# The Vector engine's order in a Mamba-style layer with a following feed-forward layer: the bias of B and C moved ahead of both weightings of x

## The chip, the cores and the metric

One core of one Trainium2 chip. The time is device time in microseconds (us) of the whole kernel. Engines: PE (TensorE), DVE (VectorE), ACT (ScalarE), POOL (GpSimd), SP (the queue that issues DMAs here).

## What is computed

The input is x of shape (8, 512, 128), fp32. Two residual blocks follow each other:

```
x = x + layernorm(attn(layernorm(x)))
x = x + layernorm(ffn(layernorm(x)))

attn: proj = x @ W_in  ->  z (256), x_raw (512), B (2*64), C (64), dt, lambda, theta
      x_raw = silu(x_raw);  B, C = rms(B)*bias_B, rms(C)*bias_C;  B, C rotated by cumulated angles
      xg = lam*dt * x_raw           (own token)
      xb = (1-lam)*dt*alpha * x_raw of the token before
      chunked state-space sum over 32 heads: scores C.B inside a chunk, a carried state between chunks
      y = rms(y * silu(z));  out = y @ W_out
ffn:  token-shift mixes of x; r = sigmoid(xr@W_r), k = relu(xk@W_k)**2, out = r * (k@W_v)
```

## The kernel before, in words

The eight sequences are cut into chunks of 64 tokens, and two sequences share the 128 partitions, so the work is 32 tiles: tile n is chunk n // 4 of the pair n % 4. A tile depends on tile n-4 through the carried state `st`. The order on each engine is written out by hand: each engine runs its own program, one `step(n, ...)` after the other from n = -2 (PE from -1) to 31, and the engines meet only through semaphores. Steps of different tiles are interleaved: in step n the core of tile n is computed, while tiles n+1 and n+2 are prepared and tile n-1 is finished. The feed-forward block of the chunk two to four back is spread over the steps as well (the functions called `ffn`).

**PE in step n** (lines 1163 to 1182): `project_x(n + 1)` (three matmuls of 512 columns, line 859, into bank 1 `x_ps`; it waits until DVE has made `xg` of tile n from that bank), `turn(n + 1)` (line 923; transposes the rotated B and C, and waits for `mask(n)` of DVE), `project_bc(n + 2)` (three matmuls of 448 columns, line 851, into bank 0 `zbc_ps`: B, C, z), `y_turn(n - 1)` (line 1045; waits for DVE's `y` and, through `o_sb`, for ACT's `late_o` of tile n-2), `mix(n)` (lines 946, 952, 958; needs `x1` and `xg` of tile n), `score(n + 1)` (line 937), `y_out(n - 1)` (line 1054), and a part of the feed-forward block.

**ACT in step n** (lines 700 to 717): `late_o(n - 2)` (lines 686, 688), `x_gate(n + 1)` (line 660: silu of `x_ps` in place, as soon as line 859 is through), `turned(n + 1)`, `copy_in(n + 3)`, a part of the feed-forward block, `late_yt(n - 1)` (line 676), `squares(n + 2)` (lines 649, 651: the sums of squares of B and C; it waits for `bc_ready` of tile n+2, so that ACT and DVE do not read bank 0 at once), `rstd_of`, `z_gate(n + 2)` (line 666), `late_ysq(n - 1)`; then `ffn`, for n % 4 = 1 the four `normed` of line 724.

**POOL in step n**: `lower_part(n + 3)`, a part of the feed-forward block, `early(n + 2)` (lines 450, 453: from the sums of squares to the reciprocal root), `token_factors(n + 2)` (line 461: the factors `wx` of both weightings), `decayed_z(n + 2)` (line 468), `state(n)` (line 476).

**DVE in step n** (lines 1552 to 1571, where the change is): `mask(n)` (line 1378), `gated_y(n - 1)` (line 1397), `state(n - 1)` (line 1386), a part of the feed-forward block, then the first weighting of x of tile n+1 (`x1`, line 1371, which waits for the silu of line 660 and for `wx`), the bias of B and C of tile n+2 (`bc`, line 1354, which waits for line 851), the second weighting of tile n+1 (`xg`, line 1371, the same bank, no further wait), and `rotations(n + 2)` (lines 1359 and 1364). The bias of tile 0 runs before all steps. Between the first steps stand pieces of the preparation: after step 0 `sine_cosine_angles(1)` (lines 1312, 1315, 1316), after step 2 `mixing_weights` (lines 1344 to 1350), and before step 4 a wait for ACT's last sines (line 1589).

Two branches of the program exist; the inputs take `tiles(False)`. After tile 31 the rest of the feed-forward block runs alone (`last_ffn`).

Of the kernel before, what the change touches and what calls it, by code (L numbers as in the profile page):

```python
# [86 lines left out]
def build(nc, x, w_in, a_log, dt_bias, bc_bias, w_out, w_r, w_k, w_v, mu, consts, out, force_general=False):  # L87
    ctx = ExitStack()
    with ctx:  # L89
# [122 lines left out]
        def within(n):  # L212

            return not isinstance(n, int) or 0 <= n < NT
# [15 lines left out]
        def carries(i):  # L230

            return not isinstance(i, int) or i < NT - NQ
# [76 lines left out]
        def lo(u):  # L309
            return UNITS[u][0]  # L310
# [22 lines left out]
        def n_of(u):  # L333
            return hi(u) - lo(u)
# [8 lines left out]
        def column2(i):  # L343

            return i // NQ % 2 * 2 * NQ + i % NQ

        def column3(i):
            return column2(i) + NQ
# [4 lines left out]
        for u2, u3 in ((7, -1), (8, -1), (-1, 5), (-1, 6), (-1, 7), (-1, 8)):  # L353
            first, n = (column2(lo(u2)), n_of(u2)) if u2 >= 0 else (column3(lo(u3)), n_of(u3))
# [845 lines left out]
        def _(dve):  # L1200
# [151 lines left out]
            def biased(n):  # L1352
                dve.wait_ge(S["zbc_ps"], n + 1)
                vec.tensor_tensor(bc[:], zbc_ps[:, 0:G3 * N], bcb_sb[:], ALU.mult).then_inc(S["bc_ready"], 1)  # L1354

            def rotations(n, q):
                dve.wait_ge(S["bc_ready"], n + 1)

                vec.tensor_tensor(rot[:], bc[:].rearrange("p (g a n) -> p g a n", g=G3, a=2).unsqueeze(3)  # L1359
                                  .broadcast_to([128, G3, 2, 2, H]),  # L1360
                                  at(cs_all, n).rearrange("p (a j n) -> p a j n", a=2, j=2).unsqueeze(1)
                                  .broadcast_to([128, G3, 2, 2, H]), ALU.mult).then_inc(S["rotated"], 1)
                dve.wait_ge(S["rotated"], n + 1)
                vec.tensor_tensor(turned_bc[:, q].rearrange("p g (j n) -> p g j n", j=2), rot[:, :, 0], rot[:, :, 1],
                                  ALU.add).then_inc(S["bc_turned"], 1)

            def weighted_x(n, par, a):
                if a == 0:
                    dve.wait_ge(S["x_silu"], n + 1)
                    dve.wait_ge(S["w_ready"], n + 1)  # L1370
                vec.tensor_tensor((x1, xg)[a][:, par].rearrange("p (a e) -> p a e", e=P),  # L1371
                                  x_ps[:].rearrange("p (a e) -> p a e", e=P),
                                  wx[:, par, a].unsqueeze(2).broadcast_to([128, H * R, P]),
                                  ALU.mult).then_inc(S[("x1_ready", "xg_ready")[a]], 1)

            def mask(n):
                dve.wait_ge(S["sg_ps"], n + 1)
                vec.tensor_tensor(sg[:], scores.unsqueeze(1).broadcast_to([128, 2, R, L]),
                                  c_("masks").rearrange("p (a m) -> p a m", a=2).unsqueeze(2)
                                  .broadcast_to([128, 2, R, L]), ALU.mult).then_inc(S["sg_ready"], 1)  # L1380

            def state(i, q):
                dve.wait_ge(S["p_ps"], i + 1)
                dve.wait_ge(S["sg_ps"], i + 2)
                dve.wait_ge(S["st_ready"], i)
                vec.tensor_tensor(sp[:], p_ps, st[:, q], ALU.add).then_inc(S["p_added"], 1)  # L1386

            def gated_y(n, q, par, general):
                dve.wait_ge(S["y_ps"], n + 1)
                dve.wait_ge(S["zec_ready"], n + 1)  # L1390
                if not isinstance(n, int) or n >= 2:
                    dve.wait_ge(S["yt_ps"], n - 1)
                    dve.wait_ge(S["ysq_done"], n - 1)
                if general:
                    vec.tensor_tensor(yk[:], y_ps[par], yk[:], ALU.add).then_inc(G["own"], 1)
                    dve.wait_ge(G["own"], n + 1)
                vec.tensor_tensor(y[:, par], yk[:] if general else y_ps[par], zs[:, q], ALU.mult).then_inc(S["y_ready"], 1)
# [98 lines left out]
            def ffn(n):  # L1496
                c, q = divmod(n, NQ)
                if q == 0 and valid(c - 2):
                    moments(c - 2)
                if q == 1 and valid(c - 2):  # L1500
                    norm_biases(c - 2)
                if q == 1 and valid(c - 4):
                    last_residual(c - 4)
                if q == 2 and valid(c - 1):
                    factor_terms(c - 1)
                if q == 2 and valid(c - 3):
                    gated_v(c - 3)
                    stats3(c - 3)
                if q == 3 and 0 <= c - 1 < NC_ - 2:
                    residual(c - 1)  # L1510
                    stats2(c - 1)
# [40 lines left out]
            def step(n, q, general):  # L1552
                if within(n) and not general:
                    mask(n)
                if within(n - 1):
                    if general:
                        tokens_general(n - 1, (q - 1) % NQ, (q + 1) % 2)
                    gated_y(n - 1, (q - 1) % NQ, (q + 1) % 2, general)
                    if not general and carries(n - 1):
                        state(n - 1, (q - 1) % NQ)  # L1560
                if within(n) and general:
                    mask(n)
                ffn(n)
                if within(n + 1):
                    weighted_x(n + 1, (q + 1) % 2, 0)
                if within(n + 2) and not (isinstance(n, int) and n == -2):
                    biased(n + 2)
                if within(n + 1):
                    weighted_x(n + 1, (q + 1) % 2, 1)
                if within(n + 2):  # L1570
                    rotations(n + 2, (q + 2) % NQ)

# [2 lines left out]
            def tiles(general):  # L1575
                token_weights(0)
                dve.wait_ge(s2, CS_FIRST)
                step(-2, NQ - 2, general)
                whole_turns(1)
                step(-1, NQ - 1, general)  # L1580
                token_weights(1)
                step(0, 0, general)
                sine_cosine_angles(1)
                step(1, 1, general)
                dve.wait_ge(s2, CS_HALF)
                step(2, 2, general)
                mixing_weights()
                step(3, 3, general)
                dve.wait_ge(s2, TABLES_AT)
                for n in range(NQ, NT):  # L1590
                    step(n, n % NQ, general)
                    if n == NT - 2:
                        residual(6)
                last_ffn(general)
# [37 lines left out]
```

## Time and profile before

| | |
|---|---|
| median of 3 runs | 243.73 us (243.07, 243.73, 243.78) |
| profiled execution | 243.37 us, span 241.5 us |
| busy: PE / PE weight loads | 214.8 us (89%) / 161.2 us (67%) |
| busy: DVE / ACT / POOL | 204.0 us (84%) / 179.7 us (74%) / 140.9 us (58%) |
| mean granted PE clock | 0.969 of 2.4 GHz |
| tiles 0 to 31 on PE | about 43 to 215 us of the span |

Times in the trace count from the start of the span; what lies around the span is 243.37 - 241.5 = 1.87 us. Matmul records overlap each other, so an end is start plus duration, and the next one often starts before it. On DVE too the next instruction starts some 0.08 us before the end of the one before it.

### The profile page before, as it was taken

How to read it: one execution, taken by the hardware profiler on the slowest of the kernel's cores; microseconds unless marked ns; L12 is line 12 of the kernel's file. 1: busy time of each engine (PE TensorE's matmuls, PEld its weight loads, DVE VectorE, ACT ScalarE, POOL GpSimd, SP SyncE). 2: the span in 40 equal slices, each digit the busy share in tenths (PEclk: the TensorE clock that was granted, in tenths of full speed). 3: DMA queues.
4: the chain of work that ended last, by engine and by line, in shares of the span. 5: the costliest groups of instructions: out<-in, count | busy, mean ns of one | idle time of the engine just before them, and what ended most of it. 6: DMA issues, size and time to landing. Idle time of an engine off the chain costs nothing. (4 is left out here: it accounts for less than half of the span.)

```text
span 241.5 us, 6529 instructions
## 1 busy us (share of the span) xinstructions
PE 214.8 (89%) x1962; PEld 161.2 (67%) x1962; DVE 204.0 (84%) x646; ACT 179.7 (74%) x696; POOL 140.9 (58%) x243
## 2 busy tenths in 40 slices
PE   0896897599999999999999999999999999999930
PEld 0893442357677767768876886887687768757920
DVE  1789999987977997885999899989989996965880
ACT  2366866739988688877978799779779977969671
POOL 7344043756667778756667675867575765545430
PEclk9999799979999999999999999999999999999985
DMA  5990000000000000000000002000100100010123
GB/s 116 231 291 7 3 0 0 1 0 4 3 1 4 0 3 0 4 1 3 0 5 0 3 1 48 3 0 3 45 4 0 29 18 4 1 43 3 43 51 91
DMA packets 10199, 6.45 MB, mean 27 GB/s; under 512 B 864, under 2 KB 9856, under 8 KB 10160
## 3 DMA queue, kind: packets, MB, share of 16 engines
q1 hardware_dynamic: 10016, 5.77, 9.8%
q8 instruction: 18, 0.29, 0.5%
q0 software_dynamic: 144, 0.21, 0.4%
q14 instruction: 21, 0.17, 0.2%
HBM read 3.88 MB, written 2.10 MB: 25 GB/s over the span
## 5 line engine op out<-in xcount | busy, mean ns | idle before, releaser
L958 PE MATMUL bank<-x,sg 64*64 64x256 f32 x256 | 35.5, 397 | 0.0
L660 ACT ACTIVATE bank<-bank,rsn 128x512 f32<-128x512 f32 x32 | 21.1, 659 | 18.1 <-PE bank L859 18.1
L958 PE MATMUL bank<-xg,sg 64*64 64x256 f32 x256 | 33.4, 380 | 0.0
L1371 DVE TENSOR_TENSOR x<-bank,wx 128x512 f32<-128x512 f32 x32 | 21.8, 682 | 12.5 <-ACT bank L660 12.0
L946 PE MATMUL pair<-x,turned_bc 64*64 64x256 f32 x224 | 31.2, 398 | 0.0
L425 POOL TENSOR_TENSOR x_lo<-xnT_all,x_hi 128x128 fp32r<-128x128 f32 x32 | 14.8, 462 | 21.1 <-ACT x_hi L575 21.0
L453 POOL TENSOR_TENSOR rb<-mse,halfn 128x2 f32<-128x2 f32 x32 | 25.2, 788 | 2.5
L1054 PE MATMUL bank<-wo_sb,yt 128*128 128x128 f32 x128 | 22.8, 300 | 0.0
L495 POOL TENSOR_TENSOR frs<-fmo,halfn 128x8 f32<-128x8 f32 (+2 forms) x13 | 15.1, 1158 | 13.2 <-DVE fmo L1463 13.2
L649 ACT ACTIVATE junk<-bank 128x64 f32<-128x64 f32 x64 | 13.9, 228 | 11.8 <-DVE bc L1354 9.6
L958 PEld LDWEIGHTS bank<-xg,sg 64*64 64x64 f32 x256 | 18.1, 135 | 6.7 <-issue 0.7
L958 PEld LDWEIGHTS bank<-x,sg 64*64 64x64 f32 x256 | 15.5, 135 | 10.1 <-issue 6.1
L450 POOL TENSOR_TENSOR mse<-msb,eps_all 128x2 f32<-128x2 f32 x32 | 7.8, 244 | 24.4 <-ACT junk L651 24.4
L1371 DVE TENSOR_TENSOR xg<-bank,wx 128x512 f32<-128x512 f32 x32 | 21.7, 679 | 0.0
L468 POOL TENSOR_TENSOR zs<-zs,ec_all 128x256 f32<-128x256 f32 x32 | 21.4, 669 | 0.0
L952 PE MATMUL bank<-st,bt 64*64 64x256 f32 x128 | 19.8, 386 | 0.5 <-DVE o_all L1306 0.5
L859 PE MATMUL bank<-w_hi,x_hi 128*128 128x512 f32 x32 | 16.8, 526 | 3.8 <-DVE w_lo L1255 2.8
L937 PEld LDWEIGHTS pair<-bt 64*64 64x64 f32 x256 | 17.0, 133 | 4.4
L476 POOL TENSOR_TENSOR st<-sp,f_all 128x256 f32<-128x256 f32 x28 | 18.1, 645 | 2.5 <-DVE sp L1386 2.4
L1054 PEld LDWEIGHTS bank<-wo_sb,yt 128*128 128x128 f32 x128 | 16.7, 190 | 3.2 <-ACT yt L676 0.8
L937 PE MATMUL pair<-bt 64*64 64x64 f32 x256 | 18.0, 217 | 0.0
L1359 DVE TENSOR_TENSOR rot<-bc,cs_all 128x384 f32<-128x384 f32 x32 | 17.6, 549 | 0.0
(193 smaller groups left out, 726.5 us busy)
## 6 DMA issues: line engine op xcount, KB each, us to landing
x_all<-x SPq DMA_DIRECT2D x16, 128.0 KB, 3.9
out<-o_all SPq DMA_DIRECT2D x14, 128.0 KB, 2.4
cm<-consts SPq DMA_DIRECT2D x1, 640.0 KB, 6.2
w_sb<-w_in SPq DMA_DIRECT2D x1, 480.0 KB, 4.2
out<-o_all SPq DMA_DIRECT2D x4, 64.0 KB, 2.1
cm<-consts POOLq DMA_DIRECT2D x1, 128.0 KB, 4.0
wo_sb<-w_out SPq DMA_DIRECT2D x1, 128.0 KB, 4.7
bcb_sb<-bc_bias SPq DMA_DIRECT2D x1, 96.0 KB, 4.3
```

Of the source, the lines that this page charges most:

```text
L453: nc.gpsimd.tensor_tensor(rb[:, par], mse[:], halfn[:, 0:R], ALU.pow).then_inc(S["rb_ready"], 1)
L468: nc.gpsimd.tensor_tensor(zs[:, q].rearrange("p (h e) -> p h e", e=P), zs[:, q].rearrange("p (h e) -> p h e", e=P), at(ec_all, n).unsqueez ...
L476: nc.gpsimd.tensor_tensor(st[:, q].rearrange("p (h e) -> p h e", e=P), sp[:].rearrange("p (h e) -> p h e", e=P), at(f_all, i).unsqueeze(2) ...
L660: nc.scalar.activation(x_ps[:], x_ps[:], ACT.Silu, scale=rsn[:, par:par + 1]).then_inc(S["x_silu"], 1)
L859: mm = nc.tensor.matmul(x_ps[:], a[:, par], b[:, O_X:O_S], start=(k == 0), stop=(k == 2))
L937: mm = nc.tensor.matmul(scores[half(h), r], bt[half(r), par, r, half(h)], bt[half(r), par, 1 - r, half(h)], start=True, stop=True)
L946: mm = nc.tensor.matmul(p_ps[half(1 - h)], turned_bc[half(h), q, 2 * r], rx(x, r)[half(h)], start=(r == 0), stop=(r == R - 1))
L952: mm = nc.tensor.matmul(y_ps[par][half(h)], bt[half(1 - h), par, h, half(h)], state[half(1 - h)], start=True, stop=stop)
L958: mm = nc.tensor.matmul(y_ps[par][half(h)], sg[half(h), a, r], rx(x, r)[half(h)], start=start, stop=stop)
L1054: mm = nc.tensor.matmul(o_ps, yt[:, k], wo_sb[:, k], start=(k == 0), stop=(k == 1))
L1359: vec.tensor_tensor(rot[:], bc[:].rearrange("p (g a n) -> p g a n", g=G3, a=2).unsqueeze(3) .broadcast_to([128, G3, 2, 2, H]), at(cs_all, ...
L1371: vec.tensor_tensor((x1, xg)[a][:, par].rearrange("p (a e) -> p a e", e=P), x_ps[:].rearrange("p (a e) -> p a e", e=P), wx[:, par, a].unsq ...
```

## The change

In each step of DVE the bias of B and C of tile n+2 stands ahead of both weightings of x of tile n+1, and no longer between them. No instruction is added or removed, and no other engine's program changes.

```diff
@@ def step(n, q, general), DVE @@
                 ffn(n)
-                if within(n + 1):
-                    weighted_x(n + 1, (q + 1) % 2, 0)
                 if within(n + 2) and not (isinstance(n, int) and n == -2):
                     biased(n + 2)
-                if within(n + 1):
-                    weighted_x(n + 1, (q + 1) % 2, 1)
+                for a in range(2):
+                    if within(n + 1):
+                        weighted_x(n + 1, (q + 1) % 2, a)
                 if within(n + 2):
                     rotations(n + 2, (q + 2) % NQ)
```

## Rows read from the trace of the kernel before

**Rows 1.** Windows: stretch, length; busy (instructions) of PE, PEld, DVE, ACT, POOL; clock; DMA.

```profile
108.00:208.00 100.00, 100.00 (x1033) 78.61 (x1032) 91.48 (x281) 83.22 (x359) 66.77 (x120) 1.00 0.04 10
...
150.71:173.09 22.38, 22.38 (x234) 17.46 (x233) 21.31 (x67) 18.86 (x82) 15.19 (x28) 1.00 0.06 14
```

**Rows 2.** Waits of PE, 54 to 110 us: total us, times, longest.

```profile
PE pair L923 <- DVE sg L1378: 1.1, 3, 0.5
PE bank L1045 <- ACT junk_o L688: 0.4, 1, 0.4
PE bank L859 <- DVE xg L1371: 0.3, 1, 0.3
```

**Rows 3.** Waits, whole span: what DVE and ACT wait for around the change.

```profile
DVE x L1371 <- ACT bank L660: 12.0, 12, 2.7
...
ACT junk L649 <- DVE bc L1354: 9.6, 19, 1.8
```

**Rows 4.** Timeline, tile 10's step: start, duration, instruction [idle before <- releaser].

```profile
91.88 0.36 PE L851 MATMUL bank<-w_hi,x_lo 128*128 128x448 f32 x1
...
92.20 0.69 DVE L1371 TENSOR_TENSOR x<-bank,wx 128x512 f32<-128x512 f32 x1 [0.81 <-ACT bank L660]
92.81 0.35 DVE L1354 TENSOR_TENSOR bc<-bank,bcb_sb 128x192 f32<-128x192 f32 x1
```

**Rows 5.** Timeline of DVE, steps 0 and 1.

```profile
48.40 0.69 DVE L1371 TENSOR_TENSOR x<-bank,wx 128x512 f32<-128x512 f32 x1
...
49.91 0.36 DVE L1354 TENSOR_TENSOR bc<-bank,bcb_sb 128x192 f32<-128x192 f32 x1 [0.83 <-PE bank L851]
...
52.36 0.68 DVE L1315 TENSOR_SCALAR o_all<-o_all 128x512 f32<-128x512 f32 x1
52.96 1.12 DVE L1316 SCALAR_TENSOR_TENSOR o_all<-o_all 128x512 f32<-128x512 f32 x1
```

**Rows 6.** Timeline of PE, the end of project_bc(2) and turn(2).

```profile
49.30 0.57 PE L851 MATMUL bank<-w_hi,x_lo 128*128 128x448 f32 x1
...
54.56 0.41 PE L923 MATMUL pair<-cm,turned_bc 128*128 128x128 f32 x2 [0.53 <-DVE sg L1378]
```

**Rows 7.** Timeline of DVE, the same two lines in the preparation, alone.

```profile
36.04 0.43 DVE L1315 TENSOR_SCALAR o_all<-o_all 128x512 f32<-128x512 f32 x1
36.39 0.69 DVE L1316 SCALAR_TENSOR_TENSOR o_all<-o_all 128x512 f32<-128x512 f32 x1
```

**Rows 8.** Timeline of POOL beside them in step 0.

```profile
52.72 0.81 POOL L468 TENSOR_TENSOR zs<-zs,ec_all 128x256 f32<-128x256 f32 x1
```

**Rows 9.** Timeline of DVE, idle times in steps 2 to 4.

```profile
57.91 0.43 DVE L1378 TENSOR_TENSOR sg<-pair,cm 128x256 f32<-128x256 f32 x1 [0.47 <-PE pair L937]
...
59.96 0.69 DVE L1371 TENSOR_TENSOR x<-bank,wx 128x512 f32<-128x512 f32 x1 [0.97 <-ACT bank L660]
...
67.76 0.42 DVE L1378 TENSOR_TENSOR sg<-pair,cm 128x256 f32<-128x256 f32 x1 [1.04 <-ACT cs_all L635]
```

**Rows 10.** Timeline of DVE, step 6.

```profile
78.06 0.69 DVE L1371 TENSOR_TENSOR x<-bank,wx 128x512 f32<-128x512 f32 x1 [0.30 <-ACT bank L660]
```

**Rows 11.** Timeline of ACT, steps 9 and 10, and of PE behind it.

```profile
92.56 0.38 ACT L676 ACTIVATE yt<-bank 128x256 f32<-128x256 f32 x1
93.19 0.22 ACT L649 ACTIVATE junk<-bank 128x64 f32<-128x64 f32 x1 [0.25 <-DVE bc L1354]
...
96.67 0.19 ACT L688 ACTIVATION_READ_ACCUMULATOR junk_o<-bank 128x1 f32 x1
...
97.01 0.41 PE L1045 MATMUL bank<-cm,y 128*128 128x128 f32 x2 [0.39 <-ACT junk_o L688]
```

**Rows 12.** Windows of PE: stretch, length, busy us (instructions), granted clock, DMA.

```profile
38.00:39.00 1.00, 0.55 (x2) 1.00 0.00 0
...
47.00:48.00 1.00, 0.06 (x1) 1.00 0.00 0
...
50.00:51.00 1.00, 1.00 (x12) 0.50 0.00 0
```

## The prediction, made before the changed kernel was run

> **What bounds the kernel now.** I read the windows first, then the waits of PE, then the timelines around each wait. From 108 to 208 us PE is busy for 100.00 of 100.00 us at full clock, and one chunk of four tiles takes 22.38 us of which PE is busy 22.38, while DVE is busy 21.31, ACT 18.86, POOL 15.19 [rows 1]. So nearly half of the span is PE's alone: what DVE does earlier or later there costs nothing while it stays inside its slack. Outside that stretch PE does wait. Between 54 and 110 us the reader is to see three kinds of wait [rows 2]: three times for DVE's mask (1.1 us in all, the longest 0.5), once for DVE's `xg` (0.3), once for ACT's sum of squares of the output (0.4). The change can move the end only there and in the start before 54 us.
>
> DVE itself waits 12 times, 12.0 us, before `x1`, for the silu, and ACT waits 19 times, 9.6 us, for the bias before its squares [rows 3]. The change touches both waits.
>
> **What moves.** Three DVE instructions change places: x1, bc, xg become bc, x1, xg. None is added, and no DMA and nothing of the queues of SP and POOL is passed. From x1's start to bc's is 0.61 us [rows 4], from bc's start to the next 0.28 us or less (the bias lasts 0.35). If all inputs are there, bc comes 0.61 us earlier, x1 0.27 later, and xg and all behind it stay where they are. The later x1 has one reader, PE's mix one step on: x1 of tile 10 starts at 92.20 [rows 4], and that mix stands behind the transposes of 97.01 [rows 11]. Over 4 us of cover; cost zero, and if the cover were gone 0.27 us a tile.
>
> The new thing is the wait. x1 waited for the silu of tile n+1, bc waits for project_bc(n+2), which PE runs after the matmuls that the silu needs. In tile 10's step the last of its matmuls ends at 91.88 + 0.36 = 92.24, and x1 started at 92.20 [rows 4]. A bias that waits starts 0.04 us after that end: 49.30 + 0.57 = 49.87 and bc at 49.91 [rows 6, 5]. So bc would start at 92.28, 0.08 later than x1 did, and all of DVE behind it is 0.08 later. This is the pattern of the waits of [rows 3] in the full pace. Behind the waiting bc both weightings and the rotations queue, and behind them PE's next project_x and turn.
>
> **Term 1, step 0: +0.60 us.** Here the bias waits already, 0.83 us, until 49.91, and x1 of tile 1 ran at 48.40 to 49.09, inside that wait [rows 5]. After the change x1 stands behind the bias and its 0.60 us (one such start to the next) come on top. DVE then runs without a gap to the mask of tile 1, and PE waits for it: turn(2) starts at 54.56 after 0.53 us of idle time [rows 6]. So PE starts 0.60 later. There is a doubt of both signs: between them are two instructions that now take 0.68 and 1.12 us [rows 5], where the same lines took 0.43 and 0.69 in the preparation [rows 7]; POOL's `zs` runs beside them, 0.81 us from 52.72 [rows 8]. Shifted by 0.60 they meet POOL's work in another way. The lower bound: both run as when alone, 0.60 - 0.25 - 0.43 = -0.08. The upper bound: one more instruction is stretched like the worst, 0.60 + 0.43 = 1.03. I take 0.60, since POOL's two operations still fall into this stretch.
>
> The Trainium skill (SBUF, "Who interferes with whom") says that DVE and GpSimd share a pair of ports, that a DVE instruction with two SBUF inputs or in a two-port mode and a GpSimd one exclude each other, and that the second to come blocks until the first is through. The two rows agree (0.43 against 0.68, 0.69 against 1.12). By that rule, followed through in the new order, the first of three table instructions would hold back POOL's `wx`, which then holds back the second and `zs` the third, and the mask would come some 0.5 us later, so the sum would be 0.1 lower than mine.
>
> **Term 2, steps 1 to 4: +0.04.** In step 1 the bias starts right at its input, with x1 before it, so x1's 0.60 is again put behind it; it meets the 0.47 us that DVE waits for the scores before the mask at 57.91, and what is left (some 0.1) meets the 0.97 us before x1 at 59.96 [rows 9]. There the bias of tile 4 waits to 0.04 us after the old start of x1, and this goes through `mixing_weights` to the next mask, one of the three for which PE waits [rows 2]: +0.04 (bounds 0 and 0.1). In step 3 x1 is hidden in the same way and 0.60 more is put behind; the 1.04 us before the mask at 67.76 (ACT's sines) take it [rows 9]. If that cover were gone it would cost up to 0.6.
>
> **Term 3, step 6 and 7: +0.08.** x1 of tile 7 waits 0.30 us for the silu [rows 10]. The 0.08 enters, DVE has no further idle time up to xg and the mask of tile 8, and PE waits for both, 0.3 and then one of the three mask waits [rows 2]; it is one chain, so 0.08 counts once. In between stand four residual instructions beside two of POOL's, whose order may flip; I bound this by the stretch of [rows 5] less its twin, 0.25 either way: -0.17 to +0.33.
>
> **Term 4, ACT: -0.35.** PE's only wait for ACT there is 0.39 us at 97.01, ended by the sum of squares at 96.67 [rows 11]. Back from there ACT runs without a gap to the squares at 93.19, and before those it waited for the bias. The bias would now end at 92.28 + 0.35 = 92.63; ACT is still in the evacuation of 92.56 and lets the next start some 0.28 us on, at 92.84. So the squares and the whole row behind them come 0.35 earlier and PE gets 0.35 of its 0.39 (bounds 0 and 0.39). The other 18 waits of ACT for the bias shrink too, but nobody on PE waits for what follows them: PE is at 100% from 108 to 208 [rows 1]. After tile 31's bias nothing is changed.
>
> **Sum.** 0.60 + 0.04 + 0.08 - 0.35 = +0.37 us. Against the profiled execution: 243.37 + 0.37 = 243.74. That one lies 0.36 below the median, so for the median 243.73 + 0.37 = 244.1. Bounds: -0.08 + 0 - 0.17 - 0.39 = -0.64 and 1.03 + 0.1 + 0.33 - 0 = +1.46. 0.3% is 0.73 us, about what a measurement of this kernel can tell from no change; the forecast lies within it.
>
> **Rivals.** *A, slower: DVE is the pace.* If the 0.08 of each of the 12 waits reached PE, it would add 12 x 0.08 = 1.0: 244.1 + 1.0 = 245.1. It decides from the point where the slack between DVE's xg or mask and PE is under 0.08 us. Against it: PE shows no wait in 100 us [rows 1]. For it: DVE is at 21.31 of 22.38 us. Chance 0.11.
>
> *B, slower: the clock.* The idle time before turn(2) grows from 0.53 to 1.13 us. After the almost idle 47 to 48 us the granted clock was 0.50 at 50 to 51, the level of 1.2 GHz; after a second with 0.55 busy, at 38 to 39, it stayed 1.00 [rows 12]. If it fell again behind that gap for 3 to 4 us (an estimate from the mean PE clock of the windows around 50 us), half of those are lost: +1.7, 245.8. The gap alone is nearer to the harmless row. Chance 0.07. The Trainium skill (TensorE: Matmul & The Clock Gate, "What's actually happening") says that the gate's watch is free-running and does not start with the kernel; by that B could strike in some executions and not in others, which no row here can show.
>
> *C, faster: the start hides the wait.* DVE and POOL meet better (term 1 at -0.08) and ACT's gain stays: 243.73 - 0.08 + 0.04 + 0.08 - 0.35 = 243.4. For it: the stretched rows 0.68 and 1.12. Against it: POOL's two operations have to go somewhere. Chance 0.20, a quarter of it beyond 0.3%.
>
> The forecast itself has 0.62. Faster by over 0.3%: 0.06 (C's tail 0.05, else 0.01). Slower: 0.20 (A 0.10, B 0.07, the forecast's upper end 0.03). Same: the rest, 0.74. The range 243.3 to 245.2 holds C and most of A, and leaves out B, the far tails of terms 1 and 3 and some of A.
>
> **What would show it.** In the changed trace: x1's wait for the silu is gone and bc waits for line 851 about as often; bc starts 0.04 us after its last matmul; x1 of tile 1 follows bc at 50.2; PE's gap before turn(2) is 1.0 to 1.2 us instead of 0.53; the 0.39 gap before the transposes of tile 9 is under 0.1; ACT's 9.6 us before the squares fall by more than half; 108 to 208 stays without a PE gap and a chunk takes 22.38. The forecast is wrong if the gap before turn(2) does not grow, if the clock falls after 55 us, or if a chunk takes longer than 22.4 us.

## The result: slower by 0.4%, and the profile after

| | before | changed |
|---|---|---|
| median | 243.71 us, 8 runs (243.07 to 244.52) | 244.61 us, 8 runs (244.15 to 245.13) |
| profiled execution, span | 243.37 us, 241.5 us | 244.86 us, 242.6 us |
| busy DVE / POOL | 204.0 us / 140.9 us | 204.4 us / 144.3 us |

The ratio of the times is 1.0039, 95% interval 1.0025 to 1.0054: the change costs 0.9 us (0.6 to 1.3). The forecast was +0.37 us. POOL's 3.4 us more come from its reciprocal root, line 453 (25.2 us before, 28.9 now).

Of the changed kernel's page, part 1 and the groups around the change (line, engine, operation | busy, mean ns | idle before, releaser):

```profile
PE 214.5 (88%) x1962; PEld 162.1 (67%) x1962; DVE 204.4 (84%) x646; ACT 179.3 (74%) x696; POOL 144.3 (59%) x243
...
L1354 DVE TENSOR_TENSOR bc<-bank,bcb_sb 128x192 f32<-128x192 f32 x32 | 11.2, 349 | 14.4 <-PE bank L851 14.1
...
L1371 DVE TENSOR_TENSOR x<-bank,wx 128x512 f32<-128x512 f32 x32 | 21.7, 678 | 0.1
```

And its waits over the whole span (us in all, times, longest):

```profile
DVE bc L1354 <- PE bank L851: 14.1, 17, 2.7
...
ACT junk L649 <- DVE bc L1354: 2.4, 3, 1.5
```

The waits have moved as the edit says. `x1` waited for the silu 12 times, 12.0 us [rows 3], and waits no more; the bias waits in its place, 17 times, 14.1 us. ACT's wait for the bias is down from 9.6 us to 2.4. None of this is the cost. That stands in PE's timeline from 54 to 110 us, here all rows with an idle time ahead:

```profile
55.48 0.41 PE L923 MATMUL pair<-cm,turned_bc 128*128 128x128 f32 x2 [2.21 <-DVE sg L1378]
65.39 0.41 PE L923 MATMUL pair<-cm,turned_bc 128*128 128x128 f32 x2 [0.96 <-DVE sg L1378]
87.52 0.47 PE L859 MATMUL bank<-w_hi,x_hi 128*128 128x512 f32 x1 [0.64 <-DVE xg L1371]
88.71 0.41 PE L923 MATMUL pair<-cm,turned_bc 128*128 128x128 f32 x2 [0.26 <-DVE sg L1378]
```

Before, the same four waits were 0.53, 0.33, 0.33 and 0.25 us, and there was a fifth, 0.39 us for ACT [rows 2, 6, 11]. The fifth has gone. The first three have grown, the second to three times its length. Then PE has no gap again, and the chunk is a little shorter than before (22.38 us [rows 1]); windows of the changed kernel:

```profile
109.00:209.00 100.00, 100.00 (x1033) 79.06 (x1033) 89.93 (x280) 83.44 (x357) 68.28 (x119) 1.00 0.04 10
124.95:147.26 22.31, 22.31 (x234) 17.53 (x233) 20.90 (x67) 18.79 (x81) 15.65 (x28) 1.00 0.01 3
```

**A trap in this comparison.** The first gap, 2.21 us against 0.53, looks like a loss of 1.7 us, more than the whole change. It is not one. From turn(1) to turn(2) the kernel before took 54.56 - 48.52 = 6.04 us, the changed one 55.48 - 49.36 = 6.12. The clock differed: at 49 to 52 us it was 0.50 in the trace of before, and 1.00 in this one. PE was through earlier and waited for the same DVE. So I had both kernels profiled a second time, unaltered (the last experiment), and each then showed the other's pattern. Windows at 27 to 33 and 49 to 52 us (PE, PEld, DVE, ACT, POOL busy, then the clock), first the changed kernel, then the kernel before in its second profile:

```profile
27.00:33.00 6.00, 5.22 (x7) 2.13 (x7) 5.76 (x11) 2.95 (x5) 2.22 (x2) 0.50 0.01 3
49.00:52.00 3.00, 2.64 (x37) 1.97 (x39) 1.80 (x5) 1.74 (x10) 1.13 (x4) 1.00 0.00 0
```

```profile
27.00:33.00 6.00, 5.29 (x7) 2.12 (x7) 5.79 (x10) 2.74 (x4) 2.47 (x2) 0.50 0.01 3
49.00:52.00 3.00, 2.88 (x41) 2.12 (x41) 2.49 (x6) 1.87 (x10) 1.49 (x4) 1.00 0.00 0
```

I call "late" the pattern with the slow clock at 49 to 52 us and "early" the one with it at 27 to 33 us, in the preparation. (In the late one the clock is slow at 25 to 28 us too, and back at 1.00 by 29.) With four profiles the same stretches can be set side by side, all in us, starts of PE's instructions:

| | pattern | turn(1) | turn(2) | project_x(10) | project_x(17) | project_x(31) |
|---|---|---|---|---|---|---|
| before | late | 48.52 | 54.56 | 90.47 | 128.35 | 207.21 |
| before, 2nd | early | 49.12 | 54.33 | 90.23 | 128.12 | 207.01 |
| changed | early | 49.36 | 55.48 | 92.34 | 129.85 | 208.52 |
| changed, 2nd | late | 48.67 | 55.22 | 92.16 | 129.68 | 208.36 |

From turn(2) on the differences do not depend on the pattern. turn(2) to project_x(10): 35.91 and 35.90 before, 36.86 and 36.94 changed, **+0.95 to +1.04**. On to project_x(17): 37.88 and 37.89 against 37.51 and 37.52, **-0.37**. On to project_x(31): 78.86 and 78.89 against 78.67 and 78.68, **-0.2**. Only turn(1) to turn(2) must be compared within a pattern: 6.04 to 6.55 late, 5.21 to 6.12 early. Even within the late one it is loose: the four late profiles with the new order in step 0 have 6.45 to 6.89, since the bias of tile 2 comes 1.38 to 1.82 us behind turn(1), after project_bc(2) at the slow clock. From the start of that bias to turn(2) the same four have 5.06 or 5.07, as the early one has.

### The profile page after: what moved, and what is told of

It is laid out like the page before. It is cut to its first block and busy times, and to the rows that moved or that the text cites. A ratio compares the mean times of both kernels' runs of the same rounds, so it can differ in the third digit from the quotient of the medians.

```text
span 242.6 us, 6529 instructions
## 1 busy us (share of the span) xinstructions
PE 214.5 (88%) x1962; PEld 162.1 (67%) x1962; DVE 204.4 (84%) x646; ACT 179.3 (74%) x696; POOL 144.3 (59%) x243
## 2 busy tenths in 40 slices
DMA packets 10200, 6.45 MB, mean 27 GB/s; under 512 B 865, under 2 KB 9857, under 8 KB 10161
## 3 DMA queue, kind: packets, MB, share of 16 engines
q1 hardware_dynamic: 10016, 5.77, 9.9%
## 5 line engine op out<-in xcount | busy, mean ns | idle before, releaser
L958 PE MATMUL bank<-x,sg 64*64 64x256 f32 x256 | 34.6, 389 | 0.0
L453 POOL TENSOR_TENSOR rb<-mse,halfn 128x2 f32<-128x2 f32 x32 | 28.9, 902 | 2.5
L946 PE MATMUL pair<-x,turned_bc 64*64 64x256 f32 x224 | 30.3, 389 | 0.0
L1354 DVE TENSOR_TENSOR bc<-bank,bcb_sb 128x192 f32<-128x192 f32 x32 | 11.2, 349 | 14.4 <-PE bank L851 14.1
```

Source lines behind the costliest of these rows:

```text
L453: nc.gpsimd.tensor_tensor(rb[:, par], mse[:], halfn[:, 0:R], ALU.pow).then_inc(S["rb_ready"], 1)
L946: mm = nc.tensor.matmul(p_ps[half(1 - h)], turned_bc[half(h), q, 2 * r], rx(x, r)[half(h)], start=(r == 0), stop=(r == R - 1))
L958: mm = nc.tensor.matmul(y_ps[par][half(h)], sg[half(h), a, r], rx(x, r)[half(h)], start=start, stop=stop)
```

## The experiments

A time without an interval is that of one profiled run. Eight runs of the kernel before spread over 243.07 to 244.52 us, so those times settle nothing by themselves; the readings go by the traces.

**One step back in the old order.** Three kernels, each the changed one with a single step as before: step 0 as shown, step 2 (`n == 2`), step 6 (`n == 6`).

```diff
                 ffn(n)
+                first = n == 0
+                if first and within(n + 1):
+                    weighted_x(n + 1, (q + 1) % 2, 0)
                 if within(n + 2) and not (isinstance(n, int) and n == -2):
                     biased(n + 2)
-                for a in range(2):
+                for a in range(1 if first else 0, 2):
                     if within(n + 1):
```

> The changed kernel with step 0 alone in the old order (x1 of tile 1 before the bias of tile 2). Theory (x1's 0.60 us is put behind the bias's wait in step 0, and DVE is what PE waits for before turn(2)): from turn(1) to turn(2) the trace shows 6.12 us in the changed kernel with PE at full clock; here 0.4 to 0.6 less, 5.5 to 5.7, if the clock is again full between them (6.0 if it falls there, as in the kernel before). The gap before turn(4) stays at 0.96 and that before project_x(9) at 0.65. Rival (another instruction of step 0 sets the mask of tile 1, or POOL's port takes the 0.60 back): turn(1) to turn(2) stays at 6.0 to 6.2 with full clock. Time 0.4 to 0.6 us under the changed kernel, too little to tell from one look.

Measured: 243.77 us (before 243.54). turn(1) to turn(2) took 5.67 us in the late pattern, even less than the 6.04 of the kernel before. The three table instructions had L1315 at 0.43 and L1316 at 0.89 us, where before had 0.68 and 1.12 [rows 5]. The gaps 0.96 and 0.64 stayed. So step 0 carries a cost of its own; why it came out better than in the kernel before was open then, and is answered below.

> The changed kernel with step 2 alone in the old order. Theory (the earlier bias of tile 4 lets ACT and POOL run 0.4 us earlier, and POOL's wx and zs then meet mixing_weights on the shared port, which stretches lines 1347 and 1350 from 0.22 and 0.28 us to 0.42 and 0.66): both lines are back at 0.22 and 0.28, and PE's gap before turn(4) falls from 0.96 to 0.3 to 0.4. The gap before turn(2) stays as in the changed kernel. Rival (the 0.6 comes from steps 0 and 1, carried on by DVE): the gap before turn(4) stays above 0.8.

Measured: 244.12 us. The gap before turn(4) fell from 0.96 to 0.34, turn(2) to project_x(10) from 36.86 to 36.24; the other two gaps stayed (1.07 in the late pattern, 0.64). The order of step 2 alone costs 0.62 us.

> The changed kernel with step 6 alone in the old order. Theory (0.08 us of waiting for project_bc(8) plus 0.24 us that the four residuals of step 7 lose against POOL because DVE comes to them 0.08 later): the residual group of step 7 takes 1.88 us again instead of 2.12, and PE's gap before project_x(9) falls from 0.65 to 0.3. Rival (the order of step 7 itself, bias of tile 9 first, costs it): the gap stays at 0.6 and more.

Measured: 243.86 us. The gap before project_x(9) fell from 0.64 to 0.32; turn(4) kept 0.97. The group of four residual instructions (L1444) took less, first in the changed kernel, then here:

```profile
83.01 2.12 DVE L1444 SCALAR_TENSOR_TENSOR x_all<-o_all,tokc,x_all 128x128 f32<-128x128 f32 x4
```

```profile
82.50 1.88 DVE L1444 SCALAR_TENSOR_TENSOR x_all<-o_all,tokc,x_all 128x128 f32<-128x128 f32 x4
```

**Step 2 without its meeting with POOL.** In step 2 the three instructions themselves leave DVE only 0.04 us later (the bias starts 5.44 us behind turn(2), where `x1` started at 5.40). What is longer lies behind them, in `mixing_weights`. Timeline of DVE and POOL, the changed kernel:

```profile
60.92 0.36 DVE L1354 TENSOR_TENSOR bc<-bank,bcb_sb 128x192 f32<-128x192 f32 x1 [0.97 <-PE bank L851]
...
63.71 0.42 DVE L1347 TENSOR_SCALAR wv_half<-wv_sb 128x128 f32<-128x128 f32 x1
64.05 0.66 DVE L1350 TENSOR_SCALAR w_prev<-wk_sb,one_less_mu 128x128 f32<-128x128 f32 x1
64.64 0.27 DVE L1350 TENSOR_SCALAR w_prev<-wr_sb,one_less_mu 128x128 f32<-128x128 f32 x1
...
63.57 0.48 POOL L461 TENSOR_TENSOR wx<-w_all,rb 128x128 f32<-128x128 f32 x1
64.01 0.62 POOL L468 TENSOR_TENSOR zs<-zs,ec_all 128x256 f32<-128x256 f32 x1
```

and the kernel before:

```profile
60.57 0.35 DVE L1354 TENSOR_TENSOR bc<-bank,bcb_sb 128x192 f32<-128x192 f32 x1
...
62.76 0.22 DVE L1347 TENSOR_SCALAR wv_half<-wv_sb 128x128 f32<-128x128 f32 x1
62.89 0.28 DVE L1350 TENSOR_SCALAR w_prev<-wk_sb,one_less_mu 128x128 f32<-128x128 f32 x1
...
63.09 0.53 POOL L461 TENSOR_TENSOR wx<-w_all,rb 128x128 f32<-128x128 f32 x1
63.59 0.62 POOL L468 TENSOR_TENSOR zs<-zs,ec_all 128x256 f32<-128x256 f32 x1
```

Count from turn(2) (54.56 and 55.48; the second profiles differ from these by up to 0.01 us in the kernel before, and in the changed one everything stands 0.08 later). The bias of tile 4 stood at 6.01 and stands at 5.44: 0.57 earlier, since `x1` is behind it now. Through ACT's squares and POOL's root `wx` comes at 8.09 instead of 8.53, 0.44 earlier. DVE reaches L1347 at 8.23 instead of 8.20, 0.03 later. So POOL's two operations, which began beside the last of these lines only, now fall into them: L1347 takes 0.42 instead of 0.22, the first L1350 0.66 instead of 0.28. The stretch is 0.20 + 0.38 = 0.58, with the 0.03 it is 0.61 of the gap's 0.62. To separate this from everything else that the order does, one kernel keeps the bias early and holds POOL alone back, by a wait for the rotation of tile 4:

```diff
             def early(n, par):
                 pool.wait_ge(S["sq_done"], n + 1)
+                if n == 4:
+                    pool.wait_ge(S["rotated"], n + 1)
```

> The changed kernel, all steps in the new order, but POOL's early(4) waits also for the rotations of tile 4 (line 1359), so that POOL's wx and zs of tile 4 come behind mixing_weights. Nothing is changed on DVE. Theory (port): lines 1347 and 1350 take 0.22 and 0.28 us and PE's gap before turn(4) falls from 0.96 to 0.3 to 0.4, though the bias of tile 4 stays early. Rival (the stretch comes from DVE's own order or from ACT): both lines stay at 0.4 and 0.66 and the gap at 0.96.

Measured: 244.03 us; the gap before turn(4) was 0.37, the one before project_x(9) stayed 0.64. DVE and POOL (line numbers two higher):

```profile
63.35 0.22 DVE L1349 TENSOR_SCALAR wv_half<-wv_sb 128x128 f32<-128x128 f32 x1
63.49 0.28 DVE L1352 TENSOR_SCALAR w_prev<-wk_sb,one_less_mu 128x128 f32<-128x128 f32 x1
...
63.88 0.40 POOL L463 TENSOR_TENSOR wx<-w_all,rb 128x128 f32<-128x128 f32 x1
```

The bias is as early as in the changed kernel (5.53 us behind turn(2), 5.52 in that kernel's second profile) and nearly all of the cost is gone: turn(2) to turn(4) takes 9.41 us against 10.00 there and 9.28 in the kernel before. A wait added on POOL took 0.59 us off PE's gap: the cost of step 2 is the meeting of the two engines, and the order itself has 0.13 here.

**The gain alone.** The kernel before with the new order in step 9 only:

```diff
                 ffn(n)
-                if within(n + 1):
+                first = n != 9
+                if first and within(n + 1):
                     weighted_x(n + 1, (q + 1) % 2, 0)
@@ after biased(n + 2) @@
-                if within(n + 1):
-                    weighted_x(n + 1, (q + 1) % 2, 1)
+                for a in range(1 if first else 0, 2):
+                    if within(n + 1):
+                        weighted_x(n + 1, (q + 1) % 2, a)
```

> The kernel before with step 9 alone in the new order. Theory (the earlier bias of tile 11 lets ACT come 0.35 us earlier to the sum of squares that PE waits for): the gap of 0.39 before the transposes of tile 9 (about 97 us) is gone, and the gaps before turn(2), turn(4), project_x(9) are those of the kernel before (0.53, 0.33, 0.32). Rival (the gap went because PE came later, after its other waits): it stays at 0.3 to 0.4. Time 0.35 us under the kernel before, too little for one look.

Measured: 243.36 us (median of before beside it 243.70). The gap before the transposes of tile 9 is gone, project_x(10) to (17) takes 37.52, and all else is as before, the chunk of 22.37 to 22.39 too. ACT's gain is the work of that one step.

**Step -1 alone, a theory that fell.** The good 0.43 and 0.89 of the first experiment appeared with the new order in step -1, so I thought that it set them. Same edit as above, with `n != -1`.

> The kernel before with step -1 alone in the new order. Theory (the earlier bias of tile 1 moves POOL's work in steps -1 and 0 so that lines 1315 and 1316 are stretched less): line 1315 takes 0.43 instead of 0.68 and line 1316 about 0.9 instead of 1.12, and from turn(1) to turn(2) the trace shows 5.67 us instead of 6.04 with the same clock. Rival (what was seen with step 0 in the old order came from a slightly different phase of the clock): both lines stay at 0.68 and 1.12.

Measured: 243.86 us. L1315 took 0.67 and L1316 1.11, turn(1) to turn(2) 5.69 in the early pattern, the same as with step 9 alone. Step -1 does nothing.

**Only the steps that pay.** The changed kernel with `first = n in (0, 2, 6)`.

> The changed kernel with steps 0, 2 and 6 in the old order, all others new. If these three steps hold the whole loss, the gaps before turn(4) and project_x(9) are 0.33 and 0.32, from turn(1) to turn(2) 5.67, the gap at 97 us is gone and a chunk takes 22.31: 0.37 + 0.39 + 5 times 0.06 = 1.0 us under the kernel before, 242.7 by the median of 243.7. Rival (something else in the new order costs too, behind 108 us or before 43): the time is 243.5 or more though the gaps are as said.

Measured, median of 8 runs: 243.10 us against 243.70, ratio 0.9968 (0.9951 to 0.9986), so 0.6 us faster than the kernel before by the medians and 0.8 (0.3 to 1.2) by the ratio. The times alone don't rule out the expected 1.0; the trace does. The gaps are as before (0.35, 0.33, 0.26; 1.79 before turn(2), early pattern), the ACT gap is gone, the chunk takes 22.31. The terms give -0.37 - 0.2 = -0.57; the missing 0.4 was the first experiment's luck in step 0, which I had booked as a gain: turn(1) to turn(2) takes 5.69 here, the value of the old order in this pattern with POOL served first.

**The same with the waits filled.** As in the last kernel, but the table work stands inside waits of DVE that the traces show: `sine_cosine_angles(1)` ahead of the bias in step 0, `mixing_weights` ahead of the bias in step 5.

```diff
+                if n == 0:
+                    sine_cosine_angles(1)
+                if n == 5:
+                    mixing_weights()
                 if within(n + 2) and not (isinstance(n, int) and n == -2):
                     biased(n + 2)
@@ between the steps @@
-                sine_cosine_angles(1)
...
-                mixing_weights()
```

> As the one with steps 0, 2 and 6 in the old order, and two pieces of preparation moved into idle times of DVE: sine_cosine_angles(1) from behind step 0 to between x1 and the bias in step 0, and mixing_weights from behind step 2 into step 5 ahead of the bias. If DVE's queue sets turn(2) and turn(4), both gaps (0.17 left and 0.33) go: 0.5 us under the other, 242.2. If the bias of tile 2 that comes later in step 0 (50.6 for 49.9) delays ACT or PE in its turn, a new gap before project_bc(3) or project_x(3) takes it back: 242.7 or more.

Measured, median of 6 runs: **242.18 us** against 243.70, ratio 0.9932 (0.9911 to 0.9953): 1.5 us under the kernel before and 2.4 under the changed one. turn(1) to turn(2) takes 5.34 in the late pattern, and the gaps before turn(2) and turn(4) are gone. L1315 and L1316 take 0.43 and 0.95 us now: they run at 49.56 and 49.91, long before `wx` (53.21). Some of it comes back later, in PE's timeline (0.33 before; L1444 takes 2.08 here, 1.88 in the last kernel):

```profile
85.07 0.47 PE L859 MATMUL bank<-w_hi,x_hi 128*128 128x512 f32 x1 [0.81 <-DVE xg L1371]
```

**The next gap.** On top of that, `stats2` of a chunk moved to the step after, out of the one whose `xg` is late.

```diff
                 if q == 0 and valid(c - 2):
+                    if c - 2 < NC_ - 2:
+                        stats2(c - 2)
                     moments(c - 2)
@@ q == 3 @@
                     residual(c - 1)
-                    stats2(c - 1)
```

> The filled kernel with the second layernorm's statistics of chunks 0 to 5 (line 1450, 0.86 us of DVE for four tiles) moved from the fourth step of a chunk to the first of the next, behind the residuals. If DVE's queue in step 7 sets project_x(9), whose gap has grown to 0.81, that gap falls to zero, the gap of 0.25 before turn(9) with it, and some 0.8 to 1.0 us go: 241.3 by the median of 243.7 before. If the later moments make normed of step 9 late instead, a new gap before the transposes of tile 9 takes it back: 242.2.

Measured, median of 6 runs: 242.15 us against 243.67, ratio 0.9941 (0.9923 to 0.9959), so nothing beyond the last kernel. The gap of 0.81 is gone and turn(2) to project_x(10) takes 35.26 instead of 36.07, but project_x(10) to (17) takes 37.79 instead of 37.51, and project_x(31) stands at 205.94 against 206.07. The 0.28 are lost at turn(10), 0.31 of them: it starts 1.08 us behind project_x(10) instead of 0.77, since DVE, with `stats2` now ahead of it, ends its mask at 0.93 instead of 0.39. That is neither the gap that I had feared nor a gap that the timeline marks. The gap before turn(9), expected to go too, stayed (0.27). With turn(1) itself 0.37 later in this profile (48.85 against 48.48), 0.50 us is won from there to project_x(31), in one profile of each kernel; the medians don't show it, and why is open.

**The shorter chunk.** The kernel before with the new order in every fourth step from step 9 on, so with ACT's earlier row of squares once in each chunk (the edit of the step-9 kernel with `first = not (n % 4 == 1 and n >= 9)`).

> The kernel before with the new order only in the steps n = 9, 13, 17, ... 29 (n % 4 = 1, those in which ACT also makes the four normed of line 724). Theory (all that the new order gives is ACT's earlier end of that row, on which PE's transposes wait): the gap of 0.39 at 97 us is gone and a chunk takes 22.31 instead of 22.38 us, as with the new order everywhere; from project_x(10) to project_x(17) 37.5 us instead of 37.9. Rival (the 0.06 of a chunk come from the other steps, by POOL or DVE): a chunk takes 22.37 to 22.39, as with step 9 alone.

Measured: 243.19 us (before 243.67). The chunk took 22.44 to 22.47 us, longer than the 22.38 of the old order and the 22.31 of the new one: neither answer. PE shows no gap in all three. The starts of project_x settle it: from (17) to (31) all tiles take the same in the three kernels, within 0.02 us, but (20) to (21), (24) to (25) and (28) to (29), with 5.82 or 5.83 us in the kernel before, 5.76 or 5.77 in the changed one, 5.89 or 5.90 here. What differs there is the start of the transposes of tile 18 (line 1045), which wait for the sum of squares of the output (line 688), as at 97 us. The bias of tile 20, ACT's sum and PE's transposes in the kernel before, the changed one and this one (project_x(20) starts at 144.89, 146.39 and 144.64):

```profile
142.70 0.34 DVE L1354 TENSOR_TENSOR bc<-bank,bcb_sb 128x192 f32<-128x192 f32 x1
146.18 0.20 ACT L688 ACTIVATION_READ_ACCUMULATOR junk_o<-bank 128x1 f32 x1
146.52 0.41 PE L1045 MATMUL bank<-cm,y 128*128 128x128 f32 x2
```

```profile
143.69 0.33 DVE L1354 TENSOR_TENSOR bc<-bank,bcb_sb 128x192 f32<-128x192 f32 x1
147.15 0.20 ACT L688 ACTIVATION_READ_ACCUMULATOR junk_o<-bank 128x1 f32 x1
148.00 0.38 PE L1045 MATMUL bank<-cm,y 128*128 128x128 f32 x2
```

```profile
142.52 0.34 DVE L1354 TENSOR_TENSOR bc<-bank,bcb_sb 128x192 f32<-128x192 f32 x1
146.00 0.19 ACT L688 ACTIVATION_READ_ACCUMULATOR junk_o<-bank 128x1 f32 x1
146.34 0.41 PE L1045 MATMUL bank<-cm,y 128*128 128x128 f32 x2
```

In the first and the third the transposes start 0.14 and 0.15 us after ACT's sum has ended, as at 97.01 after 96.86: PE waits for it, too shortly for the timeline to mark. In the second the sum ended 0.65 earlier, and PE starts in its own time, 1.61 us behind project_x(20); the other two start 0.02 and 0.09 later than that and take 0.03 longer. So the gain belongs to step 18 (22, 26: n % 4 = 2), whose bias comes 0.51 earlier in the new order (2.70 instead of 2.19 ahead of project_x(20)). This kernel has the old order there. Its new order in step 17 only makes DVE 0.07 later in step 18 (2.12 ahead), and ACT and PE with it. All fourteen profiles fit this; no run has the new order in these steps alone.

**Both kernels again.** Nothing edited.

> The changed kernel, unaltered, profiled a second time. Theory: the place of the slow clock belongs to the execution and not to the kernel, so this profile may show either pattern: slow at 27 to 33 us, turn(1) at 49.0 to 49.5 and 6.12 from turn(1) to turn(2) as in the first, or slow at 49 to 52 us, turn(1) at 48.1 to 48.9 and 6.4 to 6.9 to turn(2). In both the gap before turn(4) is 0.96, the one before project_x(9) 0.64, and turn(2) to project_x(10) takes 36.86. Rival: the pattern belongs to the kernel's order of instructions, and this profile repeats the first.

> The kernel before, unaltered, profiled a second time. Theory: either pattern; where the slow stretch lies at 27 to 33 us, turn(1) stands some 0.85 later and turn(1) to turn(2) takes 5.69 as in the runs with an old step 0; where it lies at 49 to 52 us, 48.52 and 6.04 as in the first profile. turn(2) to project_x(10) 35.91 in both. Rival: the pattern belongs to the kernel, and this profile repeats the first: slow at 49 to 52 us.

Measured: the changed kernel 244.68 us, late pattern, turn(1) to turn(2) 6.55, gaps 1.02, 0.96, 0.64; the kernel before 243.84 us, early pattern, gaps 1.31, 0.34, 0.32 (the three before turn(2), turn(4) and project_x(9)). So the pattern belongs to the execution, and not to the order. One number missed: the kernel before took 5.21 us from turn(1) to turn(2), not 5.69. That is the good case of the first experiment once more, now without any edit, and its rows say what it is. Second profile of the kernel before, DVE and POOL in step 0:

```profile
52.62 0.43 DVE L1315 TENSOR_SCALAR o_all<-o_all 128x512 f32<-128x512 f32 x1
52.97 0.89 DVE L1316 SCALAR_TENSOR_TENSOR o_all<-o_all 128x512 f32<-128x512 f32 x1
...
52.62 0.69 POOL L461 TENSOR_TENSOR wx<-w_all,rb 128x128 f32<-128x128 f32 x1
53.27 1.07 POOL L468 TENSOR_TENSOR zs<-zs,ec_all 128x256 f32<-128x256 f32 x1
```

and the first profile, whose DVE rows are [rows 5]: L1315 at 52.36 with 0.68, L1316 with 1.12.

```profile
52.36 0.40 POOL L461 TENSOR_TENSOR wx<-w_all,rb 128x128 f32<-128x128 f32 x1
```

L1315 and `wx` start at the same hundredth of a microsecond. Who was served first is read from which of the two took as long as when alone: in the first profile POOL (`wx` 0.40, L1315 0.68), in the second DVE (`wx` 0.69, L1315 0.43). It is no accident that they meet: both count from the bias of tile 2, the one through the rotations, the other through squares and root, and both stand 2.45 us behind it in either profile (52.36 - 49.91, 52.62 - 50.17). Seven profiles have the old order in step 0 and the tables behind it; in all seven the two starts are within 0.01 us of each other, and POOL was first in five, DVE in two. DVE first is 0.48 us better for turn(2): from the start of the bias to turn(2) it is 4.16 us in the two profiles with DVE first, 4.63 to 4.65 in the five with POOL first, whatever the clock (5.21 against 5.69 from turn(1), early; 5.67 against 6.04 late, where the bias stood 0.12 later in the better one).

In the new order they don't meet so. From the first profile of the changed kernel:

```profile
50.42 0.36 DVE L1354 TENSOR_TENSOR bc<-bank,bcb_sb 128x192 f32<-128x192 f32 x1 [1.20 <-PE bank L851]
50.69 0.68 DVE L1371 TENSOR_TENSOR x<-bank,wx 128x512 f32<-128x512 f32 x1
...
53.46 0.50 DVE L1315 TENSOR_SCALAR o_all<-o_all 128x512 f32<-128x512 f32 x1
53.89 1.11 DVE L1316 SCALAR_TENSOR_TENSOR o_all<-o_all 128x512 f32<-128x512 f32 x1
...
53.07 0.62 POOL L461 TENSOR_TENSOR wx<-w_all,rb 128x128 f32<-128x128 f32 x1
```

`x1` and its 0.60 us are behind the bias on DVE alone, while on POOL only the root before `wx` is longer (L453, 1.11 instead of 0.81 us). So `wx` comes 0.39 before L1315 and has 0.23 to go when that starts; L1315 loses 0.07. All five profiles with the new order in step 0 (and the tables behind it) have 0.50 or 0.51 and 1.11 or 1.12, and 5.06 or 5.07 from the bias to turn(2).

## Why the prediction was right, and where it failed

The side and the mechanism held: DVE's starting steps lose, ACT's gap is won, the full pace is indifferent. 244.6 lies in the range. But the sum was +0.37 where +0.9 was measured, and by its terms it fares worse than by its total. That the range holds is partly luck: it was wide for the meeting in step 0, and it was another meeting, in step 2, that used the room.

**Term 1, step 0 (+0.60).** `x1` follows the bias by 0.27 us, as written, and its 0.60 came on top. Against a profile of before in which POOL is served first, L1315 gives 0.17 back: +0.43 in the early pattern (6.12 against 5.69), +0.51 in the late one (6.55 against 6.04; there the bias itself stands 0.09 later behind turn(1)), and +0.42 in both from the bias on (5.06 against 4.64). Against one in which DVE is first it costs 5.21 to 6.12, +0.91. The bounds of -0.08 and 1.03 held both. The prediction's estimate by the rule of the Trainium skill (SBUF — State Buffer, "Who interferes with whom"), that a VectorE instruction and a GpSimd one that need the shared ports exclude each other, was 0.5 for this term; the measured 0.43 is nearer to that than to 0.60. The same section says that issue order and not the shape of the operation decides who blocks; the trace agrees (0.43 and 0.69 us one way, 0.68 and 0.40 the other).

**Term 2, steps 1 to 4 (+0.04): the step that failed.** The prediction said of the 0.04 that "this goes through `mixing_weights` to the next mask" and bounded it by 0 and 0.1. The 0.04 was right in the first profile (bias of tile 4 at 5.44 behind turn(2), old `x1` at 5.40); in the second it was 0.12. But the working followed DVE's queue only. That the bias comes 0.57 earlier against the DVE work behind it, and with it ACT's squares and POOL's `wx` and `zs`, was not followed through, though term 1 had just such a meeting in its rows. Measured: +0.62 (0.71 in the second profile), of which 0.58 is stretch, shown by the kernel with the old step 2 and by the one that held POOL back. It is what the sum lacked (0.9 - 0.37 = 0.5); with POOL first in step 0 the misses of the other terms nearly cancel. Even term 3's bound of 0.33 would have been too small for it. The cover of step 3 shrank as foreseen and held: 0.44 us of the 1.04 before the mask are left, at 69.30.

**Term 3, steps 6 and 7 (+0.08, up to +0.33).** Measured +0.32: 0.08 from the bias, 0.24 from L1444 against POOL (1.88 to 2.12). The mechanism and the upper bound were right, the value in the middle was not. The order of the two engines did flip, at the third POOL operation beside the residuals, `x_lo` (line 425). It starts 1.59 us behind L1444 in the kernel before and 1.52 in the changed one:

```profile
82.98 0.61 POOL L425 TENSOR_TENSOR x_lo<-xnT_all,x_hi 128x128 fp32r<-128x128 f32 x1
```

```profile
84.53 0.46 POOL L425 TENSOR_TENSOR x_lo<-xnT_all,x_hi 128x128 fp32r<-128x128 f32 x1
```

With the old order in step 6 it takes 0.60 to 0.62 and L1444 1.88, with the new one 0.46 and L1444 2.12, in every profile with the tables in their old place: a start 0.07 us earlier turned 0.15 us of POOL's loss into 0.24 of DVE's.

**Term 4, ACT (-0.35).** Measured -0.37, and the squares start 0.58 us after the last matmul of project_bc (94.69 against 93.74 + 0.37), no longer waiting for the bias but for ACT itself, where they stood 0.95 after it [rows 4, 11]. In addition each chunk from step 18 on is 0.06 shorter, -0.19 in all, which no term had. The prediction said that behind ACT's other 18 waits nobody on PE waits, since PE is at 100%. It does wait there, once in four tiles, too shortly for the busy share to show.

**The sum after the fact.** 0.43 to 0.91, + 0.62 + 0.32 - 0.37 - 0.19 = +0.81 to +1.29; measured +0.9 (0.6 to 1.3). If DVE is first as often as in these profiles, two times in seven, the mean is +0.95, an estimate from few profiles.

**The rivals.** A (DVE the pace) did not happen: no PE gap in 100 us, and chunks shorter. B (the clock) did not either: behind the longest gap, 2.21 us, the clock stayed 1.00, and behind 1.02 us too. C (a better meeting in step 0) was in none of the five profiles with the new order in step 0, where the two no longer start together; it was in two of the seven with the old order. Of the signs that I had named these came: the bias 0.04 after its last matmul (94.11 and 94.15), the gap before turn(2) at 1.02 in the profile with the clock of before. The 2.21 of the other would have misled, since I had not thought of the slow clock moving.

## What to carry over

Moving one instruction ahead on an in-order engine moves everything that it releases on the other engines too, and so changes what runs beside what: follow each of them to its new neighbours, at every place and not only at the one with the largest stretch. Before a gap in one trace is compared with a gap in another, compare the granted clock ahead of it, and measure from one landmark to the next; profile the same kernel twice. An engine that is busy for 100% of a stretch can still wait for less than the timeline marks; landmarks of two kernels side by side show it (5.83 against 5.77 us). Small table work belongs inside an existing wait: that brought 0.9 us (243.10 to 242.18), where the order of three instructions was worth 0.6 at its best.

## What was not expected of the hardware

- In all fourteen profiles the granted clock falls to 0.50 at 24 to 27 us. In six (early) it stays there to 32 to 34 us and doesn't fall again. In eight (late) it is back by 29 us and falls once more, at 48 to 50 us, to 51 to 53. Both patterns came with both orders. In the kernel before PE had waited 0.54, 0.75 and 1.46 us shortly before turn(1) and the clock fell; in its second profile it had waited 0.39, 0.74 and 1.46, and the clock stayed. turn(1) comes at 48.16 to 48.85 us in the late ones and 48.98 to 49.54 in the early ones. The Trainium skill (TensorE: Matmul & The Clock Gate, "What's actually happening") says that the window in which the gate watches is free-running and does not start with the kernel; by that rule two places for one program are possible, and the second profiles agree.
- Two engines that count from one event can start instructions that stretch each other within 0.01 us, in all seven profiles, and be served in either order: 0.48 us on the critical path in 243.
- DVE beside POOL's `wx` and `zs`: a 128x512 tensor_scalar took 0.43 us alone, 0.50 and 0.68 beside them; a 128x128 one 0.28 and 0.66; a 128x512 scalar_tensor_tensor 0.69, 0.89 and 1.12. Four scalar_tensor_tensor of 128x128 beside `zs`, `st` and `x_lo` took 1.88 or 2.12. POOL's `wx` took 0.40 alone and up to 0.82 beside DVE (47.47 us, the kernel before), `zs` 0.62 and up to 1.09 (48.28 us, the changed one).
